# Attention on one core: the softmax maxima taken for half a group of heads at a time, their rows transposed by four fp32 matmuls in column groups and split straight out of PSUM; w_proj loaded and ternarised ahead of W_o

## The chip, the core and the metric

The kernel runs on one core of a Trainium2 chip. The core has TensorE (PE in the profile; PEld is its weight load), VectorE (DVE), ScalarE (ACT), GpSimd (POOL) and SyncE (SP), which here only issues DMAs. The engines run their own instruction streams and meet at semaphores. The metric is the device time of one execution in microseconds; lower is better.

## The reference

x has shape (8, 1024, 512), fp32. All of it is one layer:

```python
xn = _layernorm(x, axis=-1)
x = x + _L0_attn_ref(xn, L0_attn_W_qkv, L0_attn_W_o) + _L0_ffn_ref(xn, L0_ffn_w_fc, L0_ffn_w_proj)
```

The attention has 16 heads of 32 dimensions:

```python
qkv = jnp.einsum('bld,ed->ble', x, W_qkv)
qkv = qkv.reshape(b, 3, H, L, D_H)
Q, K, V = (qkv[:, 0], qkv[:, 1], qkv[:, 2])
scores = jnp.einsum('bhqd,bhkd->bhqk', Q, K) * D_H ** (-0.5)
attn = jax.nn.softmax(scores, axis=-1)
out = jnp.einsum('bhqk,bhkd->bhqd', attn, V)
out = out.transpose(0, 2, 1, 3).reshape(b, L, D_IN)
return jnp.einsum('bld,ed->ble', out, W_o)
```

The feed-forward part is two linear layers (w_fc 2048x512, w_proj 512x2048) with an exact GELU between them; their weights are replaced by sign(round(w / mean|w|)) * mean|w| (ternary weights), and their inputs are normalised and clipped per row.

## The kernel before

The program has three stages, one after the other.

**Weight stage** (`weight_stage`, up to about 75 us). SP loads W_qkv in three DMAs, the first tile of x, w_fc in four, and then, when the transposes of W_qkv have left its buffer (`full32`), W_o into that buffer and behind it w_proj in four. ACT sums |w| (`fc_sum`, `proj_sum`) for the two means, PE adds the sums over partitions (`add_parts`), DVE makes thresholds of them (`thresholds`) and 0/1 masks of the weights in four pieces each (`fc_piece`, `proj_piece`), PE turns the masks into transposed ternary weights (`difference`: 8 matmuls for one 128x512 block) and ACT copies each block out of PSUM (`fc_out`, and the copies into `t2T`). For w_proj PE also adds one 512-column matmul per block (`column_sum`). W_o is transposed in fp32 and split into a high and a low fp16 part (`woh`, `wol`), which needs its largest absolute value first. The masks of w_proj overwrite those of w_fc.

**Token stage** (to about 1511 us): q, k, v and the feed-forward part for 16 tiles of 512 tokens. The change does not touch it.

**Attention stage** (`attention_output_stage`). The 128 pairs of batch and head are worked on in 32 groups g of 4 heads. A group has 16 units w: unit w handles query half `w // 8` (512 queries) and key rows `w % 8`, in steps of 8, for all four heads. Its work in one unit is four `scores` (each four matmuls of 32 output columns into the four column groups of PE, which run side by side: a "quartet"), four exponentials on ACT, and four fp32 `outputs` matmuls (probabilities times v, side by side too) for the unit before. Softmax needs the maximum of each query row before its exponential. So PE also computes the scores in the other orientation, one quartet per call of `max_scores` (64 per group, numbered r), and DVE takes the maximum of each (`maximum`). These run ahead of the group that needs them. When all 64 are there, DVE forms the negated maxima (`negate`), PE transposes them into rows (`maxima_rows`), DVE splits the rows into a high and a low fp16 part (`split_rows`), and SP writes these into rows 96 and 97 of the queries' operand `qT` (`load_maxima`), so that the `scores` matmuls subtract the maximum by themselves. `scores` at w = 0, h = 0 waits for these rows (`aug_loaded`).

The place of each step is set by hand: the loop `groups` runs every engine's `body(g, w)` over the same units, and small tables say at which w a step stands. `X_LATE = 13` is the unit from which the maxima belong to the group after the next, and below it to the next one; `ROWS_AT = 14` is the unit in which the rows of the next group are made. A prelude of 19 units (`body(-2, 13..15)`, `body(-1, 0..15)`) has nothing but maxima. Denominators (fp32 matmuls over probabilities or over their sum from POOL) stand in units 1 to 4 and 10 to 12. SP's queue also holds, in order of the units, transposing loads of q and k (`load_qk` at w = 0, 3, 6, 9), `load_v` at 2, `store_ot` at 3 and 10, `collect` at 4 and 12 (denominators to DRAM and back), `load_ones` at 12, and `spread` at 7 and 15 (inverses). In the last group, where no maxima are left, PE begins the output projection in the free places, four matmul quartets per unit from `PROJECT_AT = 3`; ACT and DVE prepare its input from w = 1 and w = 2.

The lines of the profile: L1205 is the quartet helper `in_columns` (its `98*32` form is `scores`, its `96*32` form `max_scores`), L1226 `outputs`, L1243 the transpose of the maxima, L1260 denominators, L1136 `maximum`, L1147 and L1149 the split, L1084 the exponential, L953 the DMAs of the maxima's rows, L959 and L961 those of `collect`, L969 those of `spread`.

## Time and profile before

| what | value |
|---|---|
| median of 3 runs | 3287.73 us (3284.68 to 3289.45) |
| the profiled execution's own time | 3288.71 us |
| its span in the profile | 3286.9 us |
| mean granted TensorE clock | 0.986 |
| PE busy | 3222.6 us (98% of the span) |
| DVE, ACT, POOL busy | 2425.5, 1996.4, 1828.7 us |
| SP's queue, kernel-wide | 304.69 MB |

The span is the time from the first to the last recorded instruction; the execution's own time is 1.8 us more. The times of one unit, of a wait or of a DMA's issue are read from the timeline of the trace, in which an engine's instructions of one line are merged, with their count, until something else comes between; a number in square brackets behind a row is the engine's idle time ahead of it and what ended it.

### The profile page before, as it was taken

To read this page: it belongs to the slowest core of one execution; us is meant where nothing else is said; L and a number is where in the kernel's file an instruction comes from. 1 tells how busy PE (TensorE), PEld (TensorE's weight loads), DVE (VectorE), ACT (ScalarE), POOL (GpSimd) and SP (SyncE) were. 2 spreads that over 40 slices of the span, in tenths; PEclk is the share of its full clock that TensorE was granted. 3 is DMA by queue.
4 is the path that set the end of the run, shared out by engine and by line. 5 is a ranking of instruction groups with operands and counts; after the bars stand their busy time and mean duration, and the time that the engine had idled before them with its cause. 6 is when DMAs were issued, how large, how long until landed. Compare 5 with 4: busy or idle time off the path is not lost.

```text
span 3286.9 us, 73574 instructions
## 1 busy us (share of the span) xinstructions
PE 3222.6 (98%) x30468; PEld 1530.8 (47%) x30468; DVE 2425.5 (74%) x3472; ACT 1996.4 (61%) x2969; POOL 1828.7 (56%) x659
## 2 busy tenths in 40 slices
PE   5999999999999999998999999999999999999999
PEld 4444444444444444442444444444444444444344
DVE  6777666666666776767888888888888888888544
ACT  5444444444444444440788888888888888888811
POOL 0333322323233333220789889888988988988900
PEclk8999999999999999997999999999999999999999
DMA  4132222222222223224343443433443343342296
GB/s 179 77 84 103 73 95 76 92 85 83 89 79 88 72 103 84 84 76 86 69 82 71 87 77 71 90 77 76 85 80 84 71 87 77 72 89 64 75 343 232
DMA packets 376191, 309.36 MB, mean 94 GB/s; under 512 B 300800, under 2 KB 317184, under 8 KB 365568
## 3 DMA queue, kind: packets, MB, share of 16 engines
q1 hardware_dynamic: 375872, 304.69, 34.6%
q8 instruction: 251, 4.11, 0.5%
q14 instruction: 68, 0.56, 0.1%
HBM read 96.99 MB, written 139.46 MB: 72 GB/s over the span
## 4 chain that ended last, share of the span: by engine, by line
PE 51%; DVE 1%; ACT 1%; DMA 0%; issue 0%; SPq 0%; DVEq 0%
PE es_for_maxima_and_scores L1205 27%; PE outputs L1226 13%; PE misc L1260 6%; PE es_for_maxima_and_scores L1301 5%; DVE half_maxima L1136 1%; ACT probs L1084 1%; PE misc L1243 0%; DMA k_stackT<-attention_scratch 0%; DMA q_stackT<-stack_scratch 0%; DVE q_stackT L1164 0%; ACT k_stackT L1095 0%; DMA q_stackT<-maxima_rows 0%; SPq L933 0%; DVE probs L1170 0%; ACT out_raw L1100 0%
## 5 line engine op out<-in xcount | busy, mean ns | idle before, releaser
L1136 DVE TENSOR_REDUCE half_maxima<-es_for_maxima_and_scores 128x1 f32<-128x512 f32 x2048 | 1274.8, 681 | 245.0 <-PE es_for_maxima_and_scores L1205 227.6
L1084 ACT ACTIVATE probs<-es_for_maxima_and_scores,scalars 128x512 f32<-128x512 f32 x2048 | 1245.9, 692 | 300.5 <-PE es_for_maxima_and_scores L1205 296.9
L1052 POOL TENSOR_TENSOR probs_sum<-probs_sum,probs 128x2048 f32<-128x2048 f32 x224 | 1027.0, 4585 | 23.8 <-ACT probs L1084 0.9
L1205 PE MATMUL es_for_maxima_and_scores<-k_stackT,q_stackT 96*32 96x512 f16 x8192 | 841.6, 389 | 11.8 <-DMA q_stackT<-stack_scratch 11.0
L1205 PE MATMUL es_for_maxima_and_scores<-q_stackT,k_stackT 98*32 98x512 f16 x8192 | 828.0, 382 | 8.3 <-ACT probs L1084 6.5
L1226 PE MATMUL outputs<-probs,v_rows 128*32 128x512 f32 x4096 | 536.1, 594 | 0.8 <-ACT probs L1084 0.8
L525 POOL TENSOR_TENSOR gelu_sum<-gelu_sum,gelu_out 128x1024 f32<-128x1024 f32 x96 | 254.5, 2651 | 451.8 <-ACT gelu_out L696 451.8
L1205 PEld LDWEIGHTS es_for_maxima_and_scores<-q_stackT,k_stackT 98*32 98x32 f16 x8192 | 321.9, 137 | 342.4 <-ACT probs L1084 108.6
L1052 POOL TENSOR_TENSOR probs_sum<-probs 128x2048 f32<-128x2048 f32 x64 | 292.9, 4577 | 213.7 <-ACT probs L1084 213.7
L1205 PEld LDWEIGHTS es_for_maxima_and_scores<-k_stackT,q_stackT 96*32 96x32 f16 x8192 | 237.0, 96 | 329.5 <-DVE half_maxima L1136 166.1
L758 PE MATMUL psA<-tile_xh,ternary_fcT 128*128 128x512 f16 x1024 | 388.2, 379 | 1.4 <-PEq L87 1.1
L770 PE MATMUL psC<-ternary_projT,h_hi 128*128 128x512 f16 x1024 | 388.1, 379 | 0.0
L758 PE MATMUL psA<-tile_xl,ternary_fcT 128*128 128x512 f16 x1024 | 388.1, 379 | 0.0
L770 PE MATMUL psC<-ternary_projT,h_lo 128*128 128x512 f16 x1024 | 388.1, 379 | 0.0
L696 ACT ACTIVATE gelu_out<-psA,scalars 128x1024 f32<-128x1024 f32 x128 | 142.5, 1113 | 345.3 <-PE psA L758 345.3
L525 POOL TENSOR_TENSOR gelu_sum<-gelu_out 128x1024 f32<-128x1024 f32 x16 | 41.0, 2566 | 515.9 <-ACT gelu_out L696 515.9
L593 DVE TENSOR_SCALAR h_hi<-gelu_out,scalars 128x1024 f16<-128x1024 f32 x128 | 186.7, 1459 | 159.3 <-ACT gelu_out L696 155.9
L734 PE MATMUL psB<-wqkvT_lo,tile_xh 128*128 128x512 f16 x768 | 291.1, 379 | 0.0
L734 PE MATMUL psB<-wqkvT_hi,tile_xh 128*128 128x512 f16 x768 | 291.1, 379 | 0.0
L676 ACT ACTIVATE hi_hi_lo_hi_rows<-psB,tile_rc 128x1024 f16<-128x1024 f32 x192 | 213.7, 1113 | 127.4 <-PE psB L734 127.4
L734 PE MATMUL psB<-wqkvT_hi,tile_xl 128*128 128x512 f16 x768 | 291.1, 379 | 0.0
L654 ACT CAST tile_xh<-psB 128x512 f16<-128x512 f32 x60 | 32.2, 589 | 314.5 <-PE psB L724 314.5
(162 smaller groups left out, 3328.0 us busy)
## 6 DMA issues: line engine op xcount, KB each, us to landing
stack_scratch<-hi_hi_lo_hi_rows SPq DMA_DIRECT2D x32, 1536.0 KB, 5.1
stack_scratch<-hi_hi_lo_hi_rows SPq DMA_DIRECT2D x32, 576.0 KB, 6.0
v_scratch<-v_rows_out SPq DMA_DIRECT2D x32, 576.0 KB, 6.9
tile_xs<-in_L_attn_x SPq DMA_DIRECT2D x16, 1024.0 KB, 4.8
x_plus_ffn_scratch<-tile_xs SPq DMA_DIRECT2D x16, 1024.0 KB, 3.9
v_rows<-v_scratch SPq DMA_DIRECT2D x32, 512.0 KB, 4.3
inverse_denominators<-denominators_scratch SPq DMA_DIRECT2D x256, 64.0 KB, 2.1
attention_scratch<-out_normed SPq DMA_DIRECT2D x64, 256.0 KB, 2.0
```

The lines of the kernel that those rows point to most:

```text
L525: nc.gpsimd.tensor_tensor(gacc[:], g[:, 0, :] if j == 1 else gacc[:], g[:, j % 4, :], ALU.add).then_inc(g_added, 1)
L593: nc.vector.tensor_scalar(hh[:, pair, :], gj, S["inv1"], None, ALU.mult).then_inc(hh_ready, 1)
L676: nc.scalar.activation(stack[:, i % 2, heads, 0:2, :], rows.unsqueeze(2).to_broadcast([P, BANK // DH, 2, DH]), ACT.Copy, scale=rc[:, s, i: ...
L734: last = nc.tensor.matmul(psB[:, u % 2, :], xx[:, s, c, i * P:(i + 1) * P], keep[ww][:, c, cols], start=(k == 0), stop=(k == len(terms) - 1))
L758: last = nc.tensor.matmul(psA[:, 2 * (j % 2) + b, :], w, xx[:, s, c, :], start=(c == 0 and k == 0), stop=(c == CD - 1 and k == 1))
L770: last = nc.tensor.matmul(psC[:, i % 2, :], h[:, f, i * P:(i + 1) * P], keep["t2T"][:, f, :], start=(f == 0 and k == 0), stop=(f == CF - 1 ...
L1052: nc.gpsimd.tensor_tensor(acc[:, hf], pr[:, 0] if j == 1 else acc[:, hf], pr[:, j], ALU.add).then_inc(added, 1)
L1084: nc.scalar.activation(pr[:, w % 8, h, :], psS[:, bank(g, HG * w + h), :], ACT.Exp, scale=keep["scal"]["escale"]).then_inc(exp_done, 1)
L1136: nc.vector.tensor_reduce(mx[:, slot(n, 2), h, t, kh:kh + 1], psX[:, bank(n, r), :], axis=AX.X, op=ALU.max).then_inc(max_done, 1)
L1205: last = nc.tensor.matmul(out[q:q + 32, :], stationary[:, q:q + 32], moving, start=start, stop=stop)
L1226: last = nc.tensor.matmul(psO[32 * h:32 * h + 32, :], v[:, slot(g, 2), h, i, :], pr[:, w % 8, h, :], start=(i == 0), stop=(i == KT_N - 1))
L1260: last = nc.tensor.matmul(psM[32 * h:32 * h + 32, :], keep["ones32"][:, 0:32], part[:, h, :], start=(k == 0), stop=(k == steps - 1))
```

## The change

Weight stage: w_proj is loaded ahead of W_o; `add_parts(0)` stands ahead of the transposes of x, `add_parts(1)` inside the blocks of w_fc (before block 11), two of ACT's sums over w_proj stand ahead of its first copies of w_fc; DVE does the thresholds of w_proj and its first pieces ahead of the maximum of W_o; PE transposes W_o after block 8 of w_proj (`output_weight`) and ACT copies it there.

Attention stage: the 64 maxima of a group are ordered by query half (`place`), `X_LATE` is 5, and rows are made for half a group at a time: for half 1 of the group itself at w = 5 (it is needed at w = 8) and for half 0 of the next group at w = 13 (needed at the next w = 0). The transpose is four fp32 matmuls with a 128x32 stationary operand, one for each head, into the four column groups; ACT makes the high part from PSUM (128x128) and DVE the low part. A half's rows go to `qT` in 8 DMAs of 4 rows of 128 values in place of 2 DMAs of 32 rows for a whole group. `scores` waits for them at w = 0 and at w = 8. The prelude is 11 units of maxima. In the last group the maxima end at w = 4, and `PROJECT_AT` is 5 (four of the projection's quartets are left for after the loop).

```diff
-            sp.wait_ge(full32, N32)
-            sp.dma_start(wo, W_o.rearrange("(j p) d -> p j d", p=P)).then_inc(ld_o, 16)
             rows = w_proj.rearrange("(j p) f -> p j f", p=P)
             for k in range(4):
                 sp.dma_start(wproj[:, k], rows[:, k]).then_inc(ld_proj[k], 16)
+            sp.wait_ge(full32, N32)
+            sp.dma_start(wo, W_o.rearrange("(j p) d -> p j d", p=P)).then_inc(ld_o, 16)
...
+            thresholds(1, S["gamma2"])
+            proj_piece(0)
+            dve.wait_ge(ld_o, 16)
+            nc.vector.tensor_reduce(sums[:, 1:2], wo, axis=AX.XY, op=ALU.max, apply_absolute_value=True).then_inc(summed, 1)
+            proj_piece(1)
             dve.wait_ge(reduced, 2)
...
-            thresholds(1, S["gamma2"])
-            proj_piece(0)
+            proj_piece(2)
+            proj_piece(3)
             dve.wait_ge(wo_scaled, 1)
...
-X_LATE = 13
+X_LATE = 5
 PER_GROUP = 2 * KT_N * HG
+PER_HALF = PER_GROUP // 2
...
-ROWS_AT = 14
+ROWS_AT = {5: (0, 1), 13: (1, 0)}
 TILES = B * L // TT
-HIGH_AT = 1
-LOW_AT = 2
-PROJECT_AT = 3
+HIGH_AT = 2
+LOW_AT = 3
+PROJECT_AT = 5
...
-            body(-2, range(X_LATE, UNITS))
             body(-1, range(UNITS))
...
-            def load_maxima(n):
-                sp.wait_ge(rows_ready, lin(n, 1, 1))
+            def load_maxima(n, hf):
+                sp.wait_ge(rows_ready, lin(n, 2, hf + 1))
                 for a in range(2):
-                    sp.dma_start(qT[STACK + a:STACK + a + 1, slot(n, 4)].rearrange("a h (t c) -> a (h t) c", c=P),
-                                 rows[:, a, :]).then_inc(aug_loaded, 16)
+                    for t in range(KT_N // 2):
+                        first = hf * BANK + t * P
+                        sp.dma_start(qT[STACK + a:STACK + a + 1, slot(n, 4), :, first:first + P],
+                                     rows[t:P:32, a, :]).then_inc(aug_loaded, 16)
...
+            def maxima_rows(n, hf):
+                act.wait_ge(a_full, lin(n, 2, hf + 1))
+                wait(act, aug_loaded, lin(n, 256, 128 * hf))
+                nc.scalar.activation(rows[:, 0, :], psM[:, 0:P], ACT.Copy, scale=1.0 / AUG_UNIT).then_inc(high_rows, 1)
...
+            def low_rows(n, hf):
+                wait(dve, aug_loaded, lin(n, 256, 128 * hf))
+                dve.wait_ge(a_full, lin(n, 2, hf + 1))
+                dve.wait_ge(high_rows, lin(n, 2, hf + 1))
+                nc.vector.scalar_tensor_tensor(rows[:, 1, :], psM[:, 0:P], 1.0 / AUG_UNIT, rows[:, 0, :],
                                                ALU.mult, ALU.subtract).then_inc(rows_ready, 1)
...
                         if x:
                             maximum(*x)
-                        if k == 0 and w == X_LATE and exists(shift(g, 1)):
-                            negate(shift(g, 1))
+                        if k == 2 and rows_due(g, w):
+                            low_rows(*rows_due(g, w))
...
                 wait(pe, exp_done, bank_free(g, HG * w + h))
+                if i == 0 and h == 0:
+                    pe.wait_ge(aug_loaded, lin(g, 256, 128 * hf + 128))
                 if w == 0 and h == 0:
-                    pe.wait_ge(aug_loaded, lin(g, 32, 32))
...
+            def maxima_rows(n, hf):
+                pe.wait_ge(nm_ready, lin(n, 2, hf + 1))
+                wait(pe, d_out, lin(n, 2, hf - 1))
+                for h in range(HG):
+                    last = nc.tensor.matmul(psM[32 * h:32 * h + 32, 0:P], nm[:, h, :], keep["id32"][:], start=True, stop=True)
+                last.then_inc(a_full, 1)
...
                     if exists(g) and exists(prev[0]):
                         outputs(*prev)
+                    if rows_due(g, w):
+                        maxima_rows(*rows_due(g, w))
                     if x[2]:
                         max_scores(*x[2])
```

On SP's queue, in one of the groups before, between `load_ones` and the end of the group (L953 are the rows of the maxima, L966 and L969 are `spread`):

```order
173 L940 DMA k_stackT<-unit_rows 2x4096
174 L959 DMA denominators_scratch<-denominators 4x512
175 L961 DMA denominators_once<-denominators_scratch 128x16
176 L953 DMA q_stackT<-maxima_rows 1x32x128 x2
177 L966 DMA denominators_scratch<-inverses_once 128x16
178 L969 DMA inverse_denominators<-denominators_scratch 32x512 x4
```

On the same queue after, from w = 4 of a group to its end (L988 is the second half of `collect`, L980 are the rows of the maxima, L958 `load_qk`):

```order
190 L988 DMA denominators_once<-denominators_scratch 128x16
191 L980 DMA q_stackT<-maxima_rows 1x4x128 x8
192 L958 DMA_TRANSPOSE k_stackT<-stack_scratch 128x1024
193 L958 DMA_TRANSPOSE q_stackT<-stack_scratch 128x1024
194 L993 DMA denominators_scratch<-inverses_once 128x16
195 L996 DMA inverse_denominators<-denominators_scratch 32x512 x4
196 L958 DMA_TRANSPOSE k_stackT<-stack_scratch 128x1024
197 L958 DMA_TRANSPOSE q_stackT<-stack_scratch 128x1024
198 L1022 DMA attention_scratch<-out_normed 128x512
199 L965 DMA k_stackT<-unit_rows 2x4096
200 L986 DMA denominators_scratch<-denominators 4x512
201 L988 DMA denominators_once<-denominators_scratch 128x16
202 L980 DMA q_stackT<-maxima_rows 1x4x128 x8
```

The two small DMAs at w = 14 have become eight at w = 5, ahead of a `load_qk` and a `spread`, and eight at w = 13, ahead of the other `spread`.

On PE before, around the transpose in unit w = 14 (the outputs are those of unit 13):

```order
3051 L1205 MATMUL scores_for_maxima_and_scores<-q_stackT,k_stackT 32x512 x4
3052 L1243 MATMUL misc<-id,negated_maxima 32x128
3053 L1226 MATMUL outputs<-probs,v_rows 32x512 x4
3054 L1205 MATMUL scores_for_maxima_and_scores<-k_stackT,q_stackT 32x512 x4
3055 L1205 MATMUL scores_for_maxima_and_scores<-q_stackT,k_stackT 32x512 x4
```

On PE after, around the rows of one half (L1243 is now the quartet helper, L1265 the outputs, L1281 the fp32 matmuls):

```order
3044 L1243 MATMUL scores_for_maxima_and_scores<-q_stackT,k_stackT 32x512 x4
3045 L1265 MATMUL outputs<-probs,v_rows 32x512 x4
3046 L1281 MATMUL misc<-id,negated_maxima 32x128 x4
3047 L1243 MATMUL scores_for_maxima_and_scores<-k_stackT,q_stackT 32x512 x4
3048 L1243 MATMUL scores_for_maxima_and_scores<-q_stackT,k_stackT 32x512 x4
```

The four matmuls stand behind the outputs of their unit, where the one transpose stood ahead of them, and there are two such places in a group.

## Rows read from the trace of the kernel before

**Rows 1.** The page: busy time of each engine, its share and instructions.
```profile
PE 3222.6 (98%) x30468; PEld 1530.8 (47%) x30468; DVE 2425.5 (74%) x3472; ACT 1996.4 (61%) x2969; POOL 1828.7 (56%) x659
```

**Rows 2.** Windows: busy us of PE, PEld, DVE, ACT, POOL, clock, DMA share, GB/s.
```profile
1520.00:1560.00 40.00, 37.87 (x260) 7.30 (x260) 38.84 (x64) 0.00 (x0) 0.00 (x0) 0.50 0.59 112
1600.00:3000.00 1400.00, 1395.05 (x20133) 669.01 (x20129) 1170.53 (x1995) 1171.81 (x1966) 1258.49 (x318) 1.00 0.39 79
1612.00:1617.00 5.00, 3.69 (x56) 1.74 (x53) 3.86 (x8) 3.53 (x7) 4.86 (x2) 1.00 0.17 26
```

**Rows 3.** Timeline of PE in the attention stage: start, us, line.
```profile
1999.72 0.42 PE L1205 MATMUL es_for_maxima_and_scores<-q_stackT,k_stackT 98*32 98x512 f16 x4
2000.08 0.29 PE L1243 MATMUL misc<-id,negated_maxima 128*32 128x128 f32 x1
2000.29 1.06 PE L1226 MATMUL outputs<-probs,v_rows 128*32 128x512 f32 x8
...
2012.47 1.03 PE L1226 MATMUL outputs<-probs,v_rows 128*32 128x512 f32 x8
2013.33 0.39 PE L1205 MATMUL es_for_maxima_and_scores<-k_stackT,q_stackT 96*32 96x512 f16 x4
...
2027.24 1.06 PE L1226 MATMUL outputs<-probs,v_rows 128*32 128x512 f32 x8
2028.75 0.42 PE L1205 MATMUL es_for_maxima_and_scores<-q_stackT,k_stackT 98*32 98x512 f16 x4
2029.85 1.06 PE L1226 MATMUL outputs<-probs,v_rows 128*32 128x512 f32 x8
```

**Rows 4.** Timeline of DVE and ACT in the same stretch.
```profile
2001.37 0.28 DVE L1149 SCALAR_TENSOR_TENSOR maxima_rows<-misc,maxima_rows 32x128 f16<-32x128 f32 x1
...
2004.45 2.42 ACT L1084 ACTIVATE probs<-es_for_maxima_and_scores,scalars 128x512 f32<-128x512 f32 x4 [0.19 <-PE es_for_maxima_and_scores L1205]
...
2013.78 2.48 DVE L1136 TENSOR_REDUCE half_maxima<-es_for_maxima_and_scores 128x1 f32<-128x512 f32 x4 [0.99 <-PE es_for_maxima_and_scores L1205]
```

**Rows 5.** DMA issues on SP by line: ns min/median/max of the issue; landing us min/median/max.
```profile
L953 SPq DMA_DIRECT2D q_stackT<-maxima_rows x64: 545/580/1466, 1565.1 to 3065.6; - x64
...
DMA to landing us min/median/max: 1.8/1.9/3.6
...
L959 SPq DMA_DIRECT2D denominators_scratch<-denominators x64: 499/543/567, 1605.0 to 3131.6; - x64
...
L961 SPq DMA_DIRECT2D denominators_once<-denominators_scratch x64: 321/340/358, 1606.7 to 3133.9; - x64
...
DMA to landing us min/median/max: 1.5/1.7/3.0
...
L969 SPq DMA_DIRECT2D inverse_denominators<-denominators_scratch x256: 302/421/1772, 1615.3 to 3156.1; - x128
```

**Rows 6.** Timeline of PE at the end of the second group.
```profile
1615.21 0.44 PE L1205 MATMUL es_for_maxima_and_scores<-q_stackT,k_stackT 98*32 98x512 f16 x4 [1.31 <-ACT probs L1084]
```

**Rows 7.** Timeline from the prelude to the first scores.
```profile
1522.51 38.95 DVE L1136 TENSOR_REDUCE half_maxima<-es_for_maxima_and_scores 128x1 f32<-128x512 f32 x65 [1.16 <-PE es_for_maxima_and_scores L1205]
...
1545.61 0.61 SPq L940 DMA_DIRECT2D k_stackT<-unit_rows  x1
...
1567.64 0.65 PE L1205 MATMUL es_for_maxima_and_scores<-q_stackT,k_stackT 98*32 98x512 f16 x4
```

**Rows 8.** Timeline of the weight stage and the token stage's first matmul.
```profile
50.01 1.98 ACT L370 ACTIVATE wqkv_rows<-wproj_rows 128x2048 f16<-128x2048 f32 x1
...
54.82 0.28 PE L324 MATMUL colsum_psum<-per_partition,ones 128*128 128x4 f32 x2
...
67.24 1.28 DVE L222 TENSOR_SCALAR wproj_rows<-wproj_rows,thresholds 128x2048 f16<-128x2048 f32 x1
...
75.17 0.38 PE L758 MATMUL psA<-tile_xh,ternary_fcT 128*128 128x512 f16 x1 [1.05 <-PEq L87]
```

**Rows 9.** Timeline of PE in the last group.
```profile
3079.37 0.40 PE L1205 MATMUL es_for_maxima_and_scores<-woT_hi,k_stackT 128*32 128x512 f16 x4 [1.74 <-DVE q_stackT L1164]
```

More of the change, by code:

```diff
@@ L298, in _ @@
                 last.then_inc(full32, 1)
-            pe.wait_ge(x2_ready, 1)
-            for c in range(CD):
-                pe.wait_ge(free32, N32)
-                for i in range(4):
-                    last = nc.tensor.transpose(ps[:, c, i * P:(i + 1) * P], x2[:, i, c * P:(c + 1) * P], id32[:])
-                last.then_inc(t_full, 1)
             def difference(u, plus, minus):
@@ L319, in column_sum, with output_weight @@
                     last.then_inc(cs_full, 1)
+            def output_weight():
+                pe.wait_ge(ld_o, 16)
+                for c in range(CD):
+                    pe.wait_ge(xl_ready, c + 1)
+                    for r in range(4):
+                        last = nc.tensor.transpose(ps[:, c, r * P:(r + 1) * P], wo[:, r, c * P:(c + 1) * P], id32[:])
+                    last.then_inc(wo_full, 1)
             def add_parts(k):
@@ L327, in _ @@
             add_parts(0)
+            pe.wait_ge(x2_ready, 1)
+            for c in range(CD):
+                pe.wait_ge(free32, N32)
+                for i in range(4):
+                    last = nc.tensor.transpose(ps[:, c, i * P:(i + 1) * P], x2[:, i, c * P:(c + 1) * P], id32[:])
+                last.then_inc(t_full, 1)
             for u in range(CF):
+                if u == SUMS_AT:
+                    add_parts(1)
                 j, c = divmod(u, CD)
@@ L333, in _ @@
                 difference(u, [above[:, 4 * j + r, cols] for r in range(4)], [fc_below[:, 4 * j + r, cols] for r in range(4)])
-            pe.wait_ge(ld_o, 16)
-            for c in range(CD):
-                pe.wait_ge(xl_ready, c + 1)
-                for r in range(4):
-                    last = nc.tensor.transpose(ps[:, c, r * P:(r + 1) * P], wo[:, r, c * P:(c + 1) * P], id32[:])
-                last.then_inc(wo_full, 1)
-            add_parts(1)
             for f in range(CF):
+                if f == 8:
+                    output_weight()
                 k, q = divmod(f, 4)
@@ L400, in _ @@
                 nc.scalar.activation(keep["woh"][:, c, :], ps[:, c, :], ACT.Copy, scale=wo_scale[:, 0:1]).then_inc(wo_hi, 1)
-            for f in range(CF):
-                act.wait_ge(full16, CF + f + 1)
-                nc.scalar.copy(keep["t2T"][:, f, :], pst[:, (CF + f) % 3, :]).then_inc(out16, 1)
+            for f in range(8, CF):
+                proj_out(f)
 def token_stage(nc, x_v, stack_dram, v_dram, yx_dram, keep):
@@ L833, in attention_output_stage @@
         mx = sb("half_maxima", [P, 2, HG, KT_N, 2])
[L834 to L835 removed]
+        nm = sb("negated_maxima", [P, HG, 32])
+        rows = sb("maxima_rows", [P, 2, P], F16)
         ones = sb("unit_rows", [2, HG * L], F16)
@@ L903, in product_bank_free, with rows_due, place @@
             return next((k + 1 for k in range(n - 1, -1, -1) if product_bank(k) == product_bank(n)), 0)
+        def rows_due(g, w):
+            if w not in ROWS_AT:
+                return None
+            ahead, hf = ROWS_AT[w]
+            n = shift(g, ahead)
+            return (n, hf) if exists(n) else None
+        def place(r):
+            hf, k = divmod(r, PER_HALF)
+            h, t, kh = k // KT_N, k % KT_N // 2, k % 2
+            return h, hf * (KT_N // 2) + t, kh
         def halves(t, i=3):
@@ L920, in maxima @@
         def maxima(g, w):
-            ahead, first = (1, w + UNITS - X_LATE) if w < X_LATE else (2, w - X_LATE)
+            ahead, first = (0, w + UNITS - X_LATE) if w < X_LATE else (1, w - X_LATE)
             n = shift(g, ahead)
@@ L1230, in max_scores @@
             def max_scores(n, r):
-                h, t, kh = r // per_head, r % per_head // 2, r % 2
-                if r % per_head == 0:
+                h, t, kh = place(r)
+                if r < PER_HALF and r % KT_N == 0:
                     pe.wait_ge(qk_loaded[slot(n, 2)][h], turn(n, 32) + 32)
@@ L1313, in _ @@
             outputs(GROUPS - 1, UNITS - 1)
+            for m in range(4 * (UNITS - PROJECT_AT), 12 * CD):
+                project(0, m // 12, m % 12)
             for k in range(DEN_STEPS[1] - 1):
```

80 lines of the change are left out of this document (34 added, 46 removed).

## The prediction

> **What bounds the kernel now.** The page first: PE is busy for 98% of the span, DVE for 74%, ACT for 61% [rows 1]. A share does not say where time can be gained or lost, so the windows come next. From 1600 to 3000 us PE is busy for 1395 of 1400 us at full clock [rows 2]: in the loop over the groups every microsecond that PE waits is a microsecond of the result. The prelude is different: from 1520 to 1560 us DVE is busy for 38.8 of 40 us while PE runs at clock 0.50, that is at the lower of its two levels [rows 2]. There DVE sets the pace, one maximum after the other.
>
> Then the timeline of PE, for the length of one unit. The outputs of two neighbouring units start at 2027.24 and 2029.85, so a plain unit takes 2.61 us; its first scores start 1.10 us ahead of its outputs (2028.75 against 2029.85), the outputs take 0.86 us (2012.47 to 2013.33), and a quartet of fp16 matmuls 0.22 us (five of them fill the 1.10) [rows 3]. ACT waits 0.19 us per unit for PE [rows 4], DVE 0.99 us in units with denominators [rows 4] and almost nothing in the others. So PE leads, ACT and DVE follow closely.
>
> **The change, part by part.**
>
> *Weight stage.* Before, ACT ends its last sum over w_proj at about 52 us (50.01 + 1.98), but PE adds the sums at 54.82, behind the transposes of W_o; DVE's last piece of w_proj ends at 68.5 (67.24 + 1.28), and the token stage's first matmul starts at 75.17 [rows 8]. After, PE adds them at once, which gives 2.8 of these 54.82 us, and ACT's sums end earlier by my estimate of some 5 us (two of them run ahead of the first copies, where ACT waits for blocks now): the thresholds come 7 to 8 us earlier. Between DVE's pieces the maximum of W_o takes the place of its low part, two steps of much the same work. So the last piece is 7 to 8 us earlier too. PE still has to do its blocks and W_o's transposes behind it. I take 7 us off. Bounds: 3 off, if PE's clock falls to its lower level for longer than it does now, and 9 off.
>
> *Prelude.* It loses 32 of its maxima. DVE does 65 in 38.95 us, 0.60 us each [rows 7], so at most 19.2 us go. But the rows of the first half need more than before. The 32 maxima of half 0 are done at 1522.5 + 32 x 0.60 = 1541.7, and the rows a few us later. SP is not free before 1546.2, since `load_ones` is issued at 1545.61 for 0.61 us, when the second group's q and k have landed [rows 7]. With eight DMAs (below) the last is issued 4.2 us later and lands after 1.9: 1552.3. The first scores start at 1567.64 now [rows 7]: 15.3 us off. I take 15, with bounds 11 (slower DMAs) and 18.
>
> *PE's own work in the loop.* The transpose costs 0.35 us now: from the quartet at 1999.72 to the outputs at 2000.29 are 0.57 us where a quartet alone takes 0.22 [rows 3]. The four matmuls run side by side; a 512-column set of the same kind (`outputs`) takes 0.86, so 128 columns take 0.22. Two sets per group replace one transpose: 2 x 0.22 - 0.35 = 0.09, times 32 is 3 us more. If a set cost 0.35 as the transpose does, 11 us more. ACT's new copy of 128x128 (a fraction of a 0.60 us exponential) fits into the 0.22 us that PE's matmuls add to its wait. DVE does 0.28 us per half where it had 0.28 and 0.27 per group. Both at nothing.
>
> *The eight DMAs, the term that decides.* The rows must be in place when `scores` of w = 8 (or of the next w = 0) starts, three units after the unit in which they are made. From the first scores of that unit: 1.10 us to the outputs, 0.86 for these, 0.22 for the four matmuls; then the third quartet of maxima, whose maximum DVE can start 0.45 us after the quartet starts (2013.33 to 2013.78) and ends 0.63 later; then the low part, 0.28 [rows 3, 4]. The rows are ready after 3.54 us. PE wants them after 3 x 2.61 + 0.22 = 8.05 us. That leaves 4.5 us for SP.
>
> Before, two DMAs of one row set each took SP 0.58 us apiece in the median, with 1.9 us from the issue to the landing [rows 5]. One issue every 0.60 us gives 0.6 + 1.9 = 2.5 us. After, there are eight: 7 x 0.60 + 1.9 = 6.1 us. **PE waits 6.1 - 4.5 = 1.6 us, twice per group**, at w = 8 in 32 groups and at w = 0 in 31: 63 x 1.6 = 101 us.
>
> How sure is 0.60? The new DMA has 4 rows of 256 bytes. The 128-row form of L961 is issued in 0.34 us, L969 in 0.42, but L959, which also takes 4 partitions that lie 32 apart, in 0.54, and L953, whose destination has the shape 1x32x128 against 1x4x128 now, in 0.58 [rows 5]. The new one is like both slow ones, so I take 0.56 and a small gap. If the two causes (few rows, three dimensions) add up, it is 0.34 + 0.20 + 0.24 = 0.78.
>
> The Trainium skill bears on this. DMA: Bandwidth & Descriptors, "Why a DMA increments its semaphore by 16 and not by 1", says that a DMA runs on as many engines, up to 16, as divide the outer dimension of both sides, and that the issuing engine writes the rest of the 16 increments itself; a 4-row DMA would run on 4 engines and leave 12 to SP. The row of L959 against that of L961 agrees; the rule gives no price of its own.
>
> What is queued behind these DMAs on SP: a `load_qk` and the `spread` of w = 7, and the `spread` of w = 15. They come up to 4 us later. POOL waits for `spread` two units after it or more; I put no term on it. That PE does not lose its clock by such a wait is seen below.
>
> *What such a wait looks like.* Before has a few. At the end of the second group the rows landed late (the longest landing is 3.6 us against 1.9 [rows 5]), and PE sat idle for 1.31 us ahead of its first scores at 1615.21, which the view puts down to ACT [rows 6]. In the window 1612 to 1617 PE is busy for 3.69 of 5 us, at clock 1.00 [rows 2]. So nothing else fills the gap, and it is lost whole.
>
> *Tail.* In the last group PE waits now for the projection's input, 1.74 us ahead of L1205 at 3079.37 [rows 9] and about as much again around it; with `PROJECT_AT` two units of 3.5 us later this goes, about 4 us. Eight more units carry maxima, in places where PE was faster without them (some 0.2 us each), and four quartets are left for after the loop (0.9 us). Together 2 us off, from 4 off to 2 more.
>
> **Sum.** 101 - 7 - 15 + 3 - 2 = 80 us, on 3288.71, the profiled execution's own time (a span of 3286.9 and 1.8 around it): 3368.7. That time is 1 us above the median of the three runs, so 3368.
>
> **Rivals.**
>
> *The rows land in time, and the kernel is faster.* If an issue takes no more than L961's 0.34 us plus a gap of 0.04 and lands as that does, in 1.7, the eight need 2.7 + 1.7 = 4.4 us, within the 4.5. Then the other terms stand alone: -21, 3267 us. It decides at a pitch of about 0.38. For it: each DMA has only 4 rows to describe. Against it: both rows of its own kind. The same page of the Trainium skill ("Anatomy of one DMA", on GpSimd's path) holds that a DMA's fixed cost is the completion and not the setup, by which eight in a row would cost little more than two; by L953's row the issue is 0.58 of 1.9. Chance 0.18.
>
> *A middle case.* With L969's 0.42 and a gap, a pitch of 0.46, the wait is 0.6: 38 - 21 = +17, 3305 us. Chance 0.10.
>
> *The issue costs add up.* A pitch of 0.80: the wait is 7 x 0.2 = 1.4 us longer, 3.0, times 63 is 189; 189 - 21 = +168, 3456 us. Chance 0.15.
>
> *PE itself is the cost.* The four fp32 matmuls at more than 0.35 us a set, with the rows in time: +11 - 24 = -13. It would not turn the sign, and is within the first rival.
>
> **How the numbers follow.** My forecast (pitch 0.54 to 0.68, a wait of 1.2 to 2.2 us, 76 to 138 us, less 21, and some 6 us for the other terms) has a chance of 0.55 and spans 3335 to 3410 by itself. The range from 3260 to 3430 takes in the first rival and the middle case and leaves out the high one, about 2 in 10. Around 0.2% (6 us) is what a measurement here can tell from no change. Faster: 0.18, the first rival. Same: 0.03, the sliver of pitches near 0.43. Slower: 0.79, the rest.
>
> **What would show it.** In the profile after: SP's line for the rows with 512 issues (8 x 64) at 0.55 to 0.60 us; idle time of PE ahead of its first scores in units 0 and 8, about 1.6 us each, and a group of about 51.4 us in place of 48.1 (16 x 2.61, 7 sets of denominators at 0.86, 0.35); clock 1.00 through the loop; first scores near 1545, after 7 us less in the weight stage and 15 less in the prelude; the token stage's first matmul near 68. An issue of 0.38 us or less, or rows that are ready much sooner than 3.5 us into their unit, makes the forecast wrong. A landing longer than 1.9 us makes it too low.

## The result, and the profile after

The changed kernel takes 3325.67 us (median of 4 runs, 3323.84 to 3326.91), the kernel before 3286.44 beside it (4 runs, 3284.68 to 3289.45). The ratio is 1.0119, with an interval of 1.0107 to 1.0131: 39 us slower. The forecast was 3368, 80 us slower, with a range from 3260 to 3430.

The page of the changed kernel, the same busy lines as [rows 1]:

```profile
span 3322.1 us, 75272 instructions
PE 3216.5 (97%) x30948; PEld 1612.4 (49%) x30948; DVE 2431.0 (73%) x3505; ACT 2022.1 (61%) x3033; POOL 1831.3 (55%) x659
```

The windows that answer to [rows 2] (busy us of PE, PEld, DVE, ACT, POOL, then clock, DMA share, GB/s):

```profile
1520.00:1560.00 40.00, 35.98 (x360) 11.66 (x360) 34.77 (x60) 14.80 (x24) 8.19 (x2) 0.64 0.56 113
1600.00:3000.00 1400.00, 1356.90 (x19844) 721.06 (x19840) 1136.72 (x1953) 1152.04 (x1951) 1220.12 (x308) 1.00 0.38 77
```

PE's clock is full in the loop, as before, but PE is idle for 43 of 1400 us where it was idle for 5. The view of waits says on what, in the stretch from 1600 to 3050 us (us in total, times, longest):

```profile
PE es_for_maxima_and_scores L1243 <- DMA q_stackT<-maxima_rows: 24.9, 29, 1.4
PE es_for_maxima_and_scores L1243 <- ACT probs L1111: 20.2, 29, 1.1
```

Both lines are the same stop, 58 in all, two per group. The wait has several semaphores, and half of the time the view puts it down to ACT. The run with two DMAs below settles that it is the rows.

The timeline, where each of the sum's terms can be read. First the weight stage and the token stage (against [rows 8]), then the prelude (against [rows 7]):

```profile
59.51 1.28 DVE L223 TENSOR_SCALAR wproj_rows<-wproj_rows,thresholds 128x2048 f16<-128x2048 f32 x1
67.51 0.38 PE L768 MATMUL psA<-tile_xh,ternary_fcT 128*128 128x512 f16 x1 [1.05 <-PEq L87]
...
1514.87 19.23 DVE L1172 TENSOR_REDUCE half_maxima<-es_for_maxima_and_scores 128x1 f32<-128x512 f32 x32 [1.29 <-PE es_for_maxima_and_scores L1243]
...
1538.12 0.61 SPq L965 DMA_DIRECT2D k_stackT<-unit_rows  x1
1538.77 4.32 SPq L980 DMA_DIRECT2D q_stackT<-maxima_rows  x8
...
1544.15 0.65 PE L1243 MATMUL es_for_maxima_and_scores<-q_stackT,k_stackT 98*32 98x512 f16 x4 [3.50 <-DMA q_stackT<-maxima_rows]
```

The token stage starts at 67.51 and not 75.17: 7.7 us earlier. (PE adds the sums over w_proj at 47.28 there and not at 54.82.) The scores start at 1544.15 and not 1567.64: 23.5 earlier, of which 15.8 come from the prelude.

Now one set of rows in the loop, from the four fp32 matmuls to the scores that need the rows:

```profile
2011.80 1.08 PE L1265 MATMUL outputs<-probs,v_rows 128*32 128x512 f32 x8
2012.66 0.43 PE L1281 MATMUL misc<-id,negated_maxima 128*32 128x128 f32 x8
2012.88 0.43 PE L1243 MATMUL es_for_maxima_and_scores<-k_stackT,q_stackT 96*32 96x512 f16 x4
...
2013.15 0.28 ACT L1127 ACTIVATE maxima_rows<-misc 128x128 f16<-128x128 f32 x1
...
2013.87 0.33 SPq L988 DMA_DIRECT2D denominators_once<-denominators_scratch  x1
2013.96 0.28 DVE L1184 SCALAR_TENSOR_TENSOR maxima_rows<-misc,maxima_rows 128x128 f16<-128x128 f32 x1
...
2014.27 4.26 SPq L980 DMA_DIRECT2D q_stackT<-maxima_rows  x8
...
2017.25 1.07 PE L1265 MATMUL outputs<-probs,v_rows 128*32 128x512 f32 x8
...
2019.68 0.44 PE L1243 MATMUL es_for_maxima_and_scores<-q_stackT,k_stackT 98*32 98x512 f16 x4 [0.70 <-DMA q_stackT<-maxima_rows]
...
2020.79 1.06 PE L1265 MATMUL outputs<-probs,v_rows 128*32 128x512 f32 x8
```

The unit's first scores start 1.10 us ahead of its outputs, at 2010.70. The rows are ready at 2014.24, after 3.54 us. SP begins at once; eight issues take 4.26 us. The last one starts 0.49 before the end of that, at 2018.04, and PE's scores follow 1.64 us later. (The view has no landing for this line, so below the last DMA is always counted like this, from the start of its issue to the start of the scores.) Between the outputs at 2017.25 and 2020.79 lie 3.54 us where 2.61 are usual: PE loses 0.93 us. The price of an issue, from the view of this line's instructions (ns min/median/max; then who waited for it), answers to L953 of [rows 5]:

```profile
L980 SPq DMA_DIRECT2D q_stackT<-maxima_rows x512: 492/492/757, 1538.8 to 3128.6; - x171
...
  PE es_for_maxima_and_scores L1243: 30.0, 33
```

An issue takes 0.49 us, and with the gap behind it one follows the other every 0.537 us (4.26 less 0.49, over 7, is 0.539).

Since the page's idle times are small sums over thousands of instructions, I use one more reading below: the distances between the starts of `outputs` from unit to unit, which are what PE's loop really costs. They are worked out from the timeline of each profiled execution, as the mean over groups 1 to 29. Distance 0 follows the first outputs of a group; distance 4 and 12 hold the fp32 matmuls, distance 6 and 14 the scores that wait for the rows, 7 and 15 what comes right behind. Distances 0 to 2, 8 to 10 are 3.47 in all kernels and 3, 5 and 11 are 2.61, but for distance 5 of the two-queue kernel (3.12).

```text
distance        4     6     7     12    13    14    15    whole group
before          2.61  2.61  2.74  2.94  2.63  2.81  3.47  48.46
after           2.83  3.70  2.62  2.83  2.61  3.54  3.47  50.25
two DMAs        2.83  2.61  2.75  2.83  2.61  2.61  3.47  48.36
six DMAs        2.83  2.74  2.73  2.83  2.61  2.62  3.47  48.49
nine DMAs       2.83  4.26  2.70  2.83  2.61  4.14  3.63  51.66
ten DMAs        2.83  4.94  2.92  2.83  2.61  4.95  4.46  54.19
high rows first 2.83  3.69  2.62  2.83  2.61  2.75  3.47  49.46
two queues      5.08  2.61  2.73  5.07  3.92  2.61  3.47  54.64
alternate       2.83  2.62  2.79  2.76  2.61  2.61  3.47  48.36
```

### The profile page after: what moved, and what is told of

It reads as the page before. It is cut to its first block, busy times and chain, and to the rows that moved or that the text cites. A ratio compares the mean times of both kernels' runs of the same rounds, so it can differ in the third digit from the quotient of the medians.

```text
span 3322.1 us, 75272 instructions
## 1 busy us (share of the span) xinstructions
PE 3216.5 (97%) x30948; PEld 1612.4 (49%) x30948; DVE 2431.0 (73%) x3505; ACT 2022.1 (61%) x3033; POOL 1831.3 (55%) x659
## 4 chain that ended last, share of the span: by engine, by line
PE 45%; SPq 4%; DMA 2%; issue 1%; ACT 1%; DVE 1%; POOL 1%; POOLq 0%; DVEq 0%
PE es_for_maxima_and_scores L1243 23%; PE outputs L1265 11%; PE misc L1295 6%; PE es_for_maxima_and_scores L1336 5%; SPq L980 3%; DMA q_stackT<-maxima_rows 2%; ACT probs L1111 1%; SPq L958 1%; POOL probs_sum L1079 1%; PE misc L1281 0%; DVE half_maxima L1172 0%; DVE maxima_rows L1184 0%; DVE q_stackT L1199 0%; DMA q_stackT<-stack_scratch 0%; DMA denominators_scratch<-denominators 0%
## 5 line engine op out<-in xcount | busy, mean ns | idle before, releaser
L1243 PE MATMUL es_for_maxima_and_scores<-q_stackT,k_stackT 98*32 98x512 f16 x8192 | 863.5, 383 | 52.4 <-DMA q_stackT<-maxima_rows 30.0
L1243 PE MATMUL es_for_maxima_and_scores<-k_stackT,q_stackT 96*32 96x512 f16 x8192 | 870.1, 386 | 12.6 <-DMA q_stackT<-stack_scratch 11.1
L1265 PE MATMUL outputs<-probs,v_rows 128*32 128x512 f32 x4096 | 543.4, 592 | 0.6 <-ACT probs L1111 0.6
L1243 PEld LDWEIGHTS es_for_maxima_and_scores<-q_stackT,k_stackT 98*32 98x32 f16 x8192 | 349.0, 137 | 352.3 <-ACT probs L1111 167.0
L1243 PEld LDWEIGHTS es_for_maxima_and_scores<-k_stackT,q_stackT 96*32 96x32 f16 x8192 | 265.6, 97 | 267.7 <-DVE half_maxima L1172 174.3
L1265 PEld LDWEIGHTS outputs<-probs,v_rows 128*32 128x32 f32 x4096 | 153.5, 110 | 146.5 <-issue 72.3
```

The lines of the kernel that those rows point to most:

```text
L1243: last = nc.tensor.matmul(out[q:q + 32, :], stationary[:, q:q + 32], moving, start=start, stop=stop)
L1265: last = nc.tensor.matmul(psO[32 * h:32 * h + 32, :], v[:, slot(g, 2), h, i, :], pr[:, w % 8, h, :], start=(i == 0), stop=(i == KT_N - 1))
```

## The experiments

All are measured beside the kernel before on the same chip, which took 3286.71 us there (3280.96 to 3288.44) in the first four and 3287.78 (3283.80 to 3290.16) in the second four. Each is the changed kernel with the edit shown, unless said otherwise. The numbers in the semaphores' waits follow the number of DMAs and are left out of the diffs.

**Two DMAs instead of eight.** Only the first of the four query blocks of a half has its rows loaded; the maxima are not taken off the scores (`ones` is zero, and the exponential's scale is a fourth, so that nothing overflows).

```diff
-                    for t in range(KT_N // 2):
+                    for t in range(1):
```

> The changed kernel with only the first of the four blocks of each row loaded, so 2 DMAs per half in place of 8; the other maxima stay out (the unit rows are 0 and the exponential's scale is a quarter, so nothing is subtracted and nothing overflows: the softmax is another one, the work the same). Theory, that the changed kernel loses 0.9 us of PE twice per group to the last of eight DMAs: rows land about 1.6 us + 0.5 after they are ready, well within the 4.5 us, PE waits nowhere at w = 0 or 8, 3325.7 - 63 x 0.94 = 3267 us (3262 to 3273). Rival, that the loss in the loop comes from the second set of matmuls, ACT's copy and the reordered maxima: the DMAs change nothing, 3320 to 3330.

Measured: 3263.85 us (3262.32 to 3264.86), ratio 0.9929 (0.9912 to 0.9945). The windows:

```profile
1600.00:3000.00 1400.00, 1400.00 (x20622) 705.95 (x20616) 1174.84 (x2027) 1188.97 (x2027) 1262.92 (x319) 1.00 0.39 79
```

PE has no idle time left in this stretch. The six further DMAs per half cost 62 us, all of the loss and more; the rest of the change is worth 23 us less than before. Half of the stops were put down to ACT, and they went as well: the view named the wrong one.

**Ten DMAs.** One more per row set, to partitions that nobody reads. The line stands behind the loop over `t`, so it makes two more for a half, ten in all.

```diff
                         sp.dma_start(qT[STACK + a:STACK + a + 1, slot(n, 4), :, first:first + P],
                                      rows[t:P:32, a, :]).then_inc(aug_loaded, 16)
+                    sp.dma_start(qT[STACK + 2 + a:STACK + 3 + a, slot(n, 4), :, first:first + P],
+                                 rows[t:P:32, a, :]).then_inc(aug_loaded, 16)
```

> The changed kernel with each of the eight DMAs issued twice, the second time to rows 98 and 99 of the same buffer, which nothing reads: 16 DMAs per half, all waited for (the label says ten, the kernel has sixteen). Theory of the DMA queue: eight more issues of 0.54 us put the last landing 4.3 us later, so 63 x 4.3 = 271 us more, 3597 us; less if the waits overlap with other late work on SP, more if SP's queue itself becomes the bound. Rival (DMAs are hidden, the compute of the rows costs): 3326 us.

This expectation works with sixteen DMAs for a half and miscounts the edit, so its 3597 says nothing of this kernel. Worked out afterwards for ten: two more issues of 0.537, 1.07 us at 63 places, 68 us, 3393. Measured: 3465.65 us (3453.2 to 3468.28), ratio 1.0546 (1.0528 to 1.0563), 140 above the changed kernel, twice as much as those 68. The least distances fit the issues: 4.59 at distance 6 where eight DMAs have 3.53, 4.54 at 14 where they have 3.47, both 1.07 longer. But distance 15, with no rows in it, grew from 3.47 to 4.46. Its timeline and windows at one such place:

```profile
2086.94 0.44 PE L1245 MATMUL es_for_maxima_and_scores<-q_stackT,k_stackT 98*32 98x512 f16 x4 [1.70 <-issue]
...
2089.78 0.71 PE L1245 MATMUL es_for_maxima_and_scores<-k_stackT,q_stackT 96*32 96x512 f16 x4
```

```profile
2086.00:2088.00 2.00, 1.06 (x20) 0.83 (x24) 0.49 (x2) 0.57 (x1) 1.22 (x1) 1.00 0.05 5
2088.00:2091.00 3.00, 3.00 (x27) 1.20 (x20) 1.41 (x3) 1.31 (x4) 0.00 (x0) 0.51 0.33 92
2091.00:2093.00 2.00, 2.00 (x32) 1.16 (x28) 1.84 (x4) 2.00 (x4) 0.00 (x0) 0.89 0.81 170
```

Behind the stop the granted clock goes to 0.51, the lower of its two levels (1.2 GHz of 2.4), for some 3 us, and a quartet takes 0.71 us and not 0.42. So this kernel pays twice: 31 x (1.24 + 1.41) = 82 us at distances 6 and 14 against eight DMAs, and 31 x (0.30 + 0.99) = 40 us behind them at 7 and 15. Together 122 of the 129 us that the spans differ by (3451.4 against 3322.1). Of the 82, 66 are the two issues; that the rest are landings that came late I only infer from distances up to 1.3 us above the least at 6, and up to 2.2 above it at 14.

**Alternate blocks, two DMAs with all rows.** A half is now every second block of 128 queries. Then the rows of its four blocks and four heads lie as 16 partitions for one strided destination, and one DMA per row set is enough, as before the change. The fp32 step is one matmul. The outputs are the reference's. The diff leaves out what follows from it: smaller tiles for the rows, the order of the maxima, and the order of the token blocks in the last stage.

```diff
-                    for t in range(KT_N // 2):
-                        first = hf * BANK + t * P
-                        sp.dma_start(qT[STACK + a:STACK + a + 1, slot(n, 4), :, first:first + P],
-                                     rows[t:P:32, a, :]).then_inc(aug_loaded, 16)
+                    blocks = qT[STACK + a:STACK + a + 1, slot(n, 4)].rearrange("a h (j f c) -> a h j f c", f=2, c=P)
+                    sp.dma_start(blocks[:, :, :, hf, :].rearrange("a h j c -> a (h j) c"), rows[:, a, :]).then_inc(aug_loaded, 16)
...
-                            qT[0:AUG, slot(g, 4), h, hf * BANK:(hf + 1) * BANK], True, True).then_inc(s_full, 1)
+                            qT[0:AUG, slot(g, 4), h].rearrange("p (j f c) -> p f j c", f=2, c=P)[:, hf], True, True).then_inc(s_full, 1)
...
-                for h in range(HG):
-                    last = nc.tensor.matmul(psM[32 * h:32 * h + 32, 0:P], nm[:, h, :], keep["id32"][:], start=True, stop=True)
-                last.then_inc(a_full, 1)
+                nc.tensor.matmul(psM[0:HG * KT_N // 2, 0:P], nm[:].rearrange("p h t -> p (h t)"), keep["id32"][:],
+                                 start=True, stop=True).then_inc(a_full, 1)
```

> The changed kernel with the query halves made of alternate blocks of 128 queries (blocks 0, 2, 4, 6 and 1, 3, 5, 7), so that the 16 rows of a half lie one stride apart in the buffer: 2 DMAs of 16 rows per half in place of 8 of 4, one fp32 matmul in place of four, same result; the token blocks of the last stage are taken in the same order. Theory: the rows land about 2.5 us after they are ready, within the 4.5 us; the waits of 63 x 0.94 = 59 us go, w = 8 gets its 0.14 us back: 3325.7 - 59 + 4 = 3270 us, below both kernels. Rival, that the loss is PE's second set and ACT's copy: 3320 to 3330. If a 16-row DMA with a strided destination is issued slower than 0.6 us, still no wait below 2 us each.

Measured: 3264.46 us (3262.41 to 3266.42), ratio 0.9933 (0.9916 to 0.9949). The stops are gone (the last line of the table above). It is faster than both kernels, and level with the kernel that leaves three quarters of the rows out. Its DMAs, by the view of their line:

```profile
L979 SPq DMA_DIRECT2D q_stackT<-maxima_rows x128: 529/583/1287, 1539.5 to 3064.1; - x128
...
DMA to landing us min/median/max: 1.7/1.7/3.5
```

Four times the rows in one DMA cost 0.58 us of issue where a quarter of them costs 0.49. Of these two, the price goes by the DMA, and hardly by what is in it.

**The weight order alone.** The kernel before with the weight stage of the changed one; on PE it reads:

```diff
             for u in range(CF):
+                if u == SUMS_AT:
+                    add_parts(1)
...
-            add_parts(1)
             for f in range(CF):
+                if f == 8:
+                    output_weight()
```

> The kernel before with the weight stage of the changed one alone. Theory, that the weight stage ends 7.7 us earlier and nothing later waits for anything else: 3286.4 - 7.7 = 3278.7 us. Rival, that the later stages give it back (the first tiles' DMAs, the clock): 3284 to 3287.

Measured: 3280.0 us (3277.16 to 3283.01, 10 runs), ratio 0.9981 (0.9972 to 0.9991), 6.7 us faster than before, where the forecast had 7.7; the rival's 3284 to 3287 is excluded.

**Six DMAs.** The fourth block's rows are not loaded, and as with two DMAs the maxima are not taken off.

```diff
-                    for t in range(KT_N // 2):
+                    for t in range(3):
```

> Changed kernel with the fourth query block's rows neither subtracted nor loaded (escale a fourth as large, so that nothing overflows; the maxima are not taken off): six DMAs on SP's queue for a half instead of eight. The theory (rows ready 3.53 us after the unit's first scores, then a DMA issued every 0.537 us, and 1.6 us from the start of the last issue to PE's first scores; PE stops where that comes later than its own work): eight stop it for about 0.94 us, six end 1.07 us earlier, so the stop is gone at both places: the pitch of the units w = 6 and w = 14 is 2.61 us, the time that of the two-DMA kernel, 3264 (3260 to 3270). The rival, that every DMA adds to the wait in proportion (transfers that compete, with no slack in front of them), takes two thirds of the way from two DMAs to eight: 3264 + 41 = 3305. The new order of DMAs, the transposes and the weights are the same in both.

Measured: 3270.16 us (3267.94 to 3270.65), ratio 0.9945 (0.9929 to 0.9962). That is just above the expected 3260 to 3270, 6 us above two DMAs, and far from the rival's 3305: six mostly fit into the slack and eight don't, so the cost has an edge and is not proportional. The 6 us are 2.3 in the prelude, where there is no slack (from the first matmul for a maximum to the first outputs 34.60 us against 32.35; four issues are 2.1), and 4 at distance 6, which is longer by 0.2 to 1.2 us in 6 of 31 groups.

**Nine DMAs.** The fourth block's low rows are also written to an unused partition, by a line behind both loops.

```diff
+                sp.dma_start(qT[STACK + 3:STACK + 4, slot(n, 4), :, first:first + P],
+                             rows[t:P:32, 1, :]).then_inc(aug_loaded, 16)
```

> Changed kernel with a ninth DMA for each half (the fourth block's low rows are also written to a partition that nobody reads). By the theory the stop at w = 6 and w = 14 grows by one issue, 0.537 us, to about 1.5 us: 63 x 0.537 = +34 on 3325.7, 3360, as long as PE's clock stays at full speed. In the ten-DMA kernel the stops were 1.08 us longer than with eight (least pitch 4.60 against 3.53 at w = 6, 4.55 against 3.47 at w = 14), but the kernel lost 140 us and not 68, and after the stop at w = 14 its matmuls ran for some 3 us at 1.2 GHz. If a stop of 1.5 us already brings the clock down behind it, the time is up to 3395 and the pitch of w = 15 is above 3.47 in most groups; if only stops of about 2 us do, it stays at 3.47. I expect the second, 3362 (3352 to 3380).

Measured: 3368.5 us (3362.62 to 3369.03), ratio 1.0241 (1.0224 to 1.0258). The stops grew by 0.56 and 0.60 us, 36 us in 31 groups, and distances 7 and 15 by 0.08 and 0.16, 7 us: 43 of the 45 us by which the spans of the profiled executions differ (3367.1 against 3322.1; the medians differ by 43). Only 5 of 62 stops brought the clock down, each of 1.9 us or more; distance 15 stayed at 3.47 in all but three groups, as expected.

**The high rows first.** The four DMAs of the high rows no longer wait for the low ones.

```diff
-                sp.wait_ge(rows_ready, lin(n, 2, hf + 1))
                 for a in range(2):
+                    sp.wait_ge((high_rows, rows_ready)[a], lin(n, 2, hf + 1))
```

> Changed kernel with the four DMAs of the high rows released by ACT's copy instead of by the DVE subtraction that follows it, so that the first four are issued before the low rows exist. Same DMAs, same outputs. At w = 13 SP is idle when ACT's copy ends, 0.8 us ahead of the subtraction, so up to 0.8 of the stop of 0.94 us goes; at w = 5 SP is held by the denominators' chain until about when the rows are ready (its issue ends 0.1 us after the subtraction), so nothing goes. Theory: the pitch of w = 14 falls from 3.5 to about 2.7 us, that of w = 6 stays at 3.6, and the time is 3325.7 - 31 x 0.8 = 3301 (3295 to 3315). Rival, that the stop hangs on the last DMA's own transfer and its landing and not on when the queue starts: no change, 3325.

Measured: 3300.62 us (3297.85 to 3301.96), ratio 1.0038 (1.0024 to 1.0052), 25 us below the changed kernel. Distance 14 fell from 3.54 to 2.75 (31 x 0.79 = 24.5), distance 6 stayed at 3.69. At w = 13 the timeline shows SP starting with ACT's copy and not behind DVE's subtraction:

```profile
2029.80 0.28 ACT L1127 ACTIVATE maxima_rows<-misc 128x128 f16<-128x128 f32 x1
2030.10 4.38 SPq L980 DMA_DIRECT2D q_stackT<-maxima_rows  x8
...
2030.62 0.28 DVE L1184 SCALAR_TENSOR_TENSOR maxima_rows<-misc,maxima_rows 128x128 f16<-128x128 f32 x1
```

The start of the queue, the number of issues and one landing make the stop; move the first, and the stop moves by as much.

**Two queues.** The high rows' DMAs are issued on ACT's queue, the low rows' on SP's.

```diff
+                act.wait_ge(high_rows, lin(n, 2, hf + 1))
+                for t in range(KT_N // 2):
+                    first = hf * BANK + t * P
+                    act.dma_start(qT[STACK:STACK + 1, slot(n, 4), :, first:first + P],
+                                  rows[t:P:32, 0, :]).then_inc(aug_loaded, 16)
```

> Changed kernel with the four DMAs of the high rows issued from ACT's queue behind its copy, the four of the low rows from SP's. Same DMAs and bytes, same outputs. If the stop comes of one queue that issues eight DMAs one after the other, four on each end 4 x 0.537 = 2.1 us earlier and the stop of 0.94 us is gone at both places: 3264 to 3270, unless ACT pays for them. ACT is busy 82% of the time in the main loop, and each issue on it may hold its instruction stream for up to the 0.54 us that one takes on SP's: 2.1 us for a half, behind which a unit's exponentials are late and PE stops for scores' banks instead; then up to 0.9 to 1.5 us come back per half, 3325 or more. The likeliest is between, 3290. Rival for the landing (transfers that slow each other, whatever the queue): no gain, 3325.

Measured: 3462.3 us (3459.87 to 3463.27), ratio 1.0529 (1.0512 to 1.0547), 137 above the changed kernel. My likeliest value, 3290, was far off. The first half of it was right: distances 6 and 14 are back at 2.61. By itself this would not show that the rows are early enough, since a new stop ahead of them (below) also puts off the time at which PE wants them. But the scores of w = 8 start 4.78 us after the last issue (median of the timeline), those of w = 0 no less than 4.76; without the stop of 2.2 us that would be 2.6, and 1.64 are needed. The price came elsewhere. The timeline of ACT and PE at one set of rows:

```profile
2079.43 0.28 ACT L1127 ACTIVATE maxima_rows<-misc 128x128 f16<-128x128 f32 x1
...
2079.74 2.29 ACTq L1131 DMA_DIRECT2D q_stackT<-maxima_rows  x4
...
2082.07 2.42 ACT L1111 ACTIVATE probs<-es_for_maxima_and_scores,scalars 128x512 f32<-128x512 f32 x4 [2.37 <-issue]
2082.81 0.65 PE L1248 MATMUL es_for_maxima_and_scores<-q_stackT,k_stackT 98*32 98x512 f16 x4 [1.92 <-ACT probs L1111]
```

ACT computes nothing for 2.37 us while it issues. No bank of scores comes free, and PE stops for nearly the whole of it: distances 4 and 12 are 2.25 and 2.24 longer. There was no slack between ACT and PE to hide it in ([rows 4] had said so: ACT waits 0.19 us per unit). And here too the clock falls behind the stop, with no DMA in it that PE waits for:

```profile
2082.00:2085.00 3.00, 2.19 (x16) 0.58 (x20) 0.30 (x1) 2.42 (x4) 2.86 (x2) 0.61 0.01 2
2085.00:2087.00 2.00, 2.00 (x32) 0.95 (x28) 1.30 (x3) 0.92 (x2) 2.00 (x1) 0.73 0.00 0
```

Behind it distance 5 is 3.12 and 13 is 3.92, where both are 2.61: 56 us in 31 groups.

## Why the prediction was right in sign and twice too large

The terms of the sum against what the profiled executions show (in us):

```text
term                                     predicted   measured
weight stage                                 -7        -7.7
prelude                                      -15       -15.8
wait for the rows, 63 places                 +101      +62.6 (31 x (1.09 + 0.93))
fp32 matmuls                                 +3        +3    (31 x 0.11, two-DMA kernel)
tail                                         -2        +2.4
work of PE hidden by the new stops            0        -4
late landings of before that are gone         0        -6
sum                                          +80       +35
```

Of the 45 us between the two sums 38 are the wait and 10 two effects that had no term; the tail goes 4 the other way. The measured 3326 lies in the range, but below the forecast's own 3335 to 3410. The spans differ by 35.2 us (3322.1 against 3286.9), so the table closes. The medians differ by 39: the profiled execution of before (3288.71) was 2 us above its median, that of after (3323.84) 2 below.

*The step that failed*, with the mechanism right and the size wrong: "PE waits 6.1 - 4.5 = 1.6 us, twice per group", with 7 x 0.60 + 1.9 = 6.1. The readiness of the rows was right (3.54 us predicted and measured), and so was the time at which PE wants them (8.05). The two prices were too high, and a small difference of large numbers takes their whole error. The pitch, the time from one issue to the next, is 0.537 and not 0.60, which takes 7 x 0.063 = 0.44 us off. From the last issue to the scores it is 1.64 and not 1.9, another 0.26. That leaves 0.89; the usual stops are 0.86 to 0.96, and a few longer ones, which I take for late landings, make the mean 1.01 and the term 62.6 us in place of 101. I had taken L953's 0.58 because its shape was nearest, and L959's 0.54 with the same 4 partitions was the better row; the landing of 1.9 was L953's with two rows of 32, while L961's 1.7 was the nearest small one. By these two rows of [rows 5], 0.54 with the gap of 0.045 seen here and 1.7, the wait would have come out as 7 x 0.585 + 1.7 - 4.5 = 1.3 us; the measured issue of 0.49 lay below the median of both rows of its kind. The same two prices show in the prelude, where eight issues take 4.32 us and the scores follow 1.55 us after the last one starts: 15.8 us off and not 15.3.

The prediction also takes the row of L959 against that of L961 as a sign that few rows cost more. The trace agrees on the count of engines: a 4-row DMA updates its semaphore 5 times (one for each of 4 engines and one for the rest would be that), those of L953 (32 rows) and L961 (128 rows) 16 times. The price doesn't follow it: 0.49 for 4 rows, 0.58 for the 16 rows of the kernel with alternate blocks and for the 32 of L953, 0.34 for L961. What sets an issue's price between 0.34 and 0.58 stays open.

*The rival "in time"* failed as argued: an issue does not cost L961's 0.34. The Trainium skill's page DMA: Bandwidth & Descriptors, "Anatomy of one DMA", says of GpSimd's path that the completion dominates the fixed cost. On SP's queue this trace agrees for a single DMA: of the 1.64 us up to the scores 0.49 are the issue. For eight in a row it is the other way about: 3.76 us pass until the last issue starts, and 1.64 after that.

*The two small effects that had no term.* Before the change, a small wait at distance 7 (0.13 us) lay on PE's path. It is gone behind the stops of the changed kernel (2.62) and back in the two-DMA kernel (2.75); I take it that the stop gives ACT its time back. 31 x 0.12 = 4 us. And stops like the one of [rows 6] stand in seven groups of before, where distance 14 is 2.9 to 4.2 us. In each of the seven the last row landed 2.4 to 3.6 us after its issue, against 1.9 in the others, and the scores start 0.11 us after that landing: it was the rows, and not ACT as the view has it. The kernel with alternate blocks still has landings of up to 3.5 us, and its distance 14 is 2.63 at most: rows that are made at w = 13 for w = 0 have slack that the one set at w = 14 had not. 31 x 0.20 = 6 us (in the profile of the weight order alone they come to 31 x 0.12 = 4, so this term varies).

*The tail.* I gave it 2 us off. The four quartets behind the loop cost 0.9 us, as worked out. But from the first outputs of the last group to its last outputs it is 50.4 us against 48.9, 1.5 more where I had 3 less: two long distances of 6.3 and 4.6 us around the projection's input have become two of 5.2 and 4.9, two units later. Moving `PROJECT_AT` moved the wait and took only 0.9 us off it, and the distances around it grew by more. What sets them there was not tried.

*ACT's copy and DVE's low part* at nothing: right. In the two-DMA kernel they are all there, and PE is busy for 1400 of 1400 us.

*The clock.* That PE doesn't lose it by such a stop held for all stops of the changed kernel, up to 1.6 us. The rival with stops of 3.0 us would probably have lost more than its 3456 said, since its sum lacked the clock: of the 123 stops over 1.95 us in the table below, 72 brought it down.

## What to carry to other kernels

Small DMAs that gate the next matmul cost their queue about one issue each here, nearly whatever they carry (0.49 us for 4 rows, 0.58 for 16): count them times the issue's time plus one landing, and set that against the time until the data is wanted. If it does not fit, first look for a layout that makes them one DMA; the same change with alternate blocks turned 39 us slower into 22 us faster, while issuing on a compute engine that runs close to the critical one cost more than the wait it removed. Where the answer is a small difference between a queue's time and a slack, give the range more trust than the value, and take prices from the nearest rows one by one.

## What the runs showed of the hardware

*Where PE's clock falls.* Over four kernels (8, 9 and 10 DMAs, two queues), at two places in each of groups 0 to 30, I read each stop as what its distance has over the usual one, and a fall as the next distance longer by over 0.3 us. The granted clock is below 1.00 behind all 76 stops with a fall, and behind no other.

```text
stop of PE, us      places   clock fell behind it
up to 1.7            114           0
1.7 to 1.95           11           4
over 1.95            123          72
```

Ahead of each, PE had worked through several units at their usual distances. A fall mostly cost 1.0 to 1.7 us more. It comes with either thing that PE waited for: rows in the ten-DMA kernel, ACT in the two-queue kernel. The length alone does not decide: of the two-queue kernel's stops of 2.15 to 2.25 us, 14 of 18 at distance 12 brought the clock down and only 2 of 21 at distance 4, and one of 2.9 us in the ten-DMA kernel did not. What else decides is not shown here. So a stop of about 2 us costs up to 3.7 in these runs, and one of 0.9 costs 0.9.

*The price of an issue.* On SP 0.49 us for 4 rows of 256 bytes and 0.58 for 16 of them, with 0.04 to 0.05 between issues. On ACT:

```profile
L1131 ACTq DMA_DIRECT2D q_stackT<-maxima_rows x256: 499/500/1102, 1536.4 to 3261.4; - x128
```

0.50 us each, and ACT's own work stands still meanwhile (2.37 us for four). With ACT issuing beside it, SP's issues of the same kind took 0.60 us in the median where they take 0.49 alone.
